# A state-space layer and an attention block on one core: reciprocals in pieces, reordered sends and earlier loads

## The reference, cut to what matters

```python
q = heads(einsum('bsh,oh->bso', x, q_weight) * q_dc)
k = heads(einsum('bsh,oh->bso', x, k_weight) * k_dc)
v = heads(einsum('bsh,oh->bso', x, v_weight) * v_dc * s2)
attn = softmax(einsum('bhqd,bhkd->bhqk', q, k) * scale)
out = einsum('bhqk,bhkd->bhqd', attn, v)          # "attended"
out = einsum('bsh,oh->bso', out, w_weight) * w_dc + skip
```

## Time and profile before

| | |
|---|---|
| three runs | 3378.05, 3388.91, 3394.20 us (median 3388.91) |
| profiled execution | 3385.69 us; its span, first to last instruction, 3383.9 us |
| PE busy | 3030.4 us (90% of the span) |
| DVE busy | 2196.9 us (65%) |
| ACT, POOL busy | 1125.4 us, 1131.3 us (33% each) |
| mean granted clock of PE | 0.909 of full speed |
| attention | about 2294 to 3256 us of the span |
| output stage | about 3256 us to the end |

### The profile page before, as it was taken

One profiled execution on the slowest core, in us unless ns is written; L12 is line 12 of the kernel. 1 busy time (PEld: TensorE's weight loads), 2 busy tenths in 40 slices (PEclk: granted clock), 3 DMA queues, 4 the chain that ended last, 5 costly groups with the idle time before them and its releaser, 6 DMA issues. The chain is left out here.

```text
span 3383.9 us, 55574 instructions
## 1 busy us (share of the span) xinstructions
PE 3030.4 (90%) x20298; PEld 1424.9 (42%) x20298; DVE 2196.9 (65%) x3117; ACT 1125.4 (33%) x1944; POOL 1131.3 (33%) x462
## 2 busy tenths in 40 slices
PE   6888875599999999999984999996999999999979
PEld 3555554234444444444432666672333333323324
DVE  3766663478898989898954334427677666666514
ACT  3645542011111111111112122213666565656620
POOL 0111111113333333333312101102666676666620
PEclk9978865578999999999996999996999999999989
DMA  2333224435555555555543333336334434353354
GB/s 68 129 110 137 90 107 137 128 79 138 143 154 146 150 144 151 144 150 145 149 141 111 128 135 142 145 116 176 83 88 102 100 93 115 73 127 90 76 190 146
DMA packets 248554, 420.82 MB, mean 124 GB/s; under 512 B 51736, under 2 KB 117912, under 8 KB 242024
## 3 DMA queue, kind: packets, MB, share of 16 engines
q1 hardware_dynamic: 202344, 385.61, 39.4%
q10 hardware_dynamic: 46080, 33.57, 4.8%
HBM read 257.82 MB, written 160.98 MB: 124 GB/s over the span
## 5 line engine op out<-in xcount | busy, mean ns | idle before, releaser
L491 DVE CUSTOM_DVE_ANT_0 b_h<-b_h,b_bx,b_bounds_all 128x256 f32<-128x256 f32 x2048 | 966.1, 535 | 145.0 <-PE b_bx L604 144.9
L1208 DVE TENSOR_REDUCE e_half_max<-ef_banks 128x4 f32<-128x2048 f32 x256 | 586.1, 2293 | 289.5 <-PE ef_banks L1161 289.5
L1342 POOL TENSOR_TENSOR e_pair_sum<-e_probs 128x2048 f32<-128x2048 f32 x128 | 585.2, 4572 | 474.7 <-PE ef_banks L1200 270.6
L1318 ACT ACTIVATE e_probs<-ef_banks 128x512 f32<-128x512 f32 x1024 | 555.8, 595 | 374.5 <-PE ef_banks L1175 374.4
L1175 PE MATMUL ef_banks<-e_qs,e_ks 97*128 97x512 f32 x1024 | 393.4, 465 | 23.1 <-DMA e_qs<-e_max_t 19.2
L614 PE MATMUL b_y_psum<-b_h,b_c_weights 128*32 128x128 f32 x8224 | 343.6, 287 | 2.4 <-ACT b_y_stage L654 2.4
L604 PE MATMUL b_bx<-b_x_moving,b_b_weights 24*128 24x512 f32 x1024 | 266.0, 514 | 56.2 <-DMA b_x_moving<-xn_parts 43.9
L1175 PEld LDWEIGHTS ef_banks<-e_qs,e_ks 97*128 97x128 f32 x1024 | 159.7, 195 | 365.3 <-ACT e_probs L1318 304.7
L525 PE MATMUL b_gate<-b_w_gate,b_x_tile 128*128 128x512 f32 x512 | 308.2, 686 | 3.7 <-DMA b_w_gate<-in_w_in_t_dram 3.7
L654 ACT COPY b_y_stage<-b_y_psum 128x128 f32<-128x128 f32 x256 | 67.9, 265 | 728.2 <-PE b_y_psum L614 726.3
L534 PE MATMUL b_p_out<-b_w_out,b_yg_t 128*128 128x512 f32 x512 | 279.1, 637 | 10.3 <-ACT b_yg_t L547 10.3
(11 more groups left out here) (183 smaller groups left out, 3273.3 us busy)
## 6 DMA issues: line engine op xcount, KB each, us to landing
b_x_moving<-xn_parts SPq DMA_DIRECT2D x256, 128.0 KB
e_ks<-qk_parts SPq DMA_DIRECT2D x48, 512.0 KB, 8.0
e_qs<-qk_parts SPq DMA_DIRECT2D x96, 256.0 KB, 11.6
xn_full<-a_xn SPq DMA_DIRECT2D x32, 512.0 KB, 2.6
xn_parts<-a_hi SPq DMA_DIRECT2D x64, 256.0 KB, 2.4
xn_parts<-a_lo SPq DMA_DIRECT2D x64, 256.0 KB, 2.4
b_x_moving<-xn_parts SPq DMA_DIRECT2D x256, 64.0 KB
silu_gate<-b_sg ACTq DMA_DIRECT2D x64, 256.0 KB, 3.6
```

The lines of the kernel that those rows point to most:

```text
L491: return nc.vector._custom_dve(bass.dve_ops.TENSOR_ADD_SAT, **operands)
L1208: nc.vector.tensor_reduce(out=half_max[:, u // UNITS % 2, :, r // NH, r % NH], in_=(banks[:, u % 2 * GROUP:(u % 2 + 1) * GROUP] if u < FIR ...
L1318: nc.scalar.activation(probs[:, g % 4, h, :], p_exp[h % 2], ACT.Exp).then_inc(exps, 1)
L1342: nc.gpsimd.tensor_tensor(out=pair_sum[:, t % 2], in0=probs[:, (2 * t) % 4], in1=probs[:, (2 * t + 1) % 4], op=ALU.add).then_inc(paired, 1)
```

## The change

Four edits.

1. The reciprocal of the sums, 512 columns in one instruction, becomes four instructions of 128 columns. The copy out of PSUM (`take_den`) stays behind unit 79 (143, 207); the pieces follow behind units 80, 81, 82 and 83. Each piece counts `den_inverted` up by one, and `store_rden` waits for all four.
2. In SP's program for a group, `send_max(2n + 2)` moves ahead of `load_rd(m + 1)` and the stores of attended values. `store_rden`, `load_rd(m)` and `send_max(2n + 1)` stay in their places.
3. The matrices of groups 0 and 1 for `max_unit` (four loads of 512 KB) are loaded in `proj_phase`, in batch 3 at `s = 8`; the attention doesn't load them or wait for them.
4. The load of attended batch 0 moves from the end of the attention into SP's program for group 15, and in `out_phase` SP waits until batch 1 has landed before it issues the loads of batches 2 and 3.

```diff
@@ proj_phase, SP
+                        if s == NQ and not ahead:
+                            for i in range(2):
+                                sp.wait_ge(qk_out[i], START + 64)
+                            for i in range(4):
+                                sp.dma_start(mats_ahead[:, i, :].bitcast(f32), QK[2 * (i % 2)].rearrange("b (g r) s -> (b g) r s", r=P)[i // 2]).then_inc(ahead_in, 16)
...
+                sp.wait_ge(ahead_in, START + 64)
@@ attention_phase
         def store_rden(sp, b):
-            sp.wait_ge(den_inverted, START + b + 1)
+            sp.wait_ge(den_inverted, START + (b + 1) * QUARTERS)
...
-            if r == 0:
-                pe.wait_ge(mats_in[i], START + (n // RING + 1) * MATS)
+            if r == 0 and n >= RING:
+                pe.wait_ge(mats_in[i], START + n // RING * MATS)
...
-        def invert(dve, b):
+        def take_den(dve, b):
             dve.wait_ge(key_sums, START + (b + 1) * LANES * NQ)
             if b:
-                dve.wait_ge(den_inverted, START + b)
+                dve.wait_ge(den_inverted, START + b * QUARTERS)
             nc.vector.tensor_copy(den[:], p_d).then_inc(den_taken, 1)
-            dve.wait_ge(den_taken, START + b + 1)
-            if b:
-                dve.wait_ge(rden_out, START + b * RDENS)
-            nc.vector.reciprocal(out=rden[:], in_=den[:]).then_inc(den_inverted, 1)
+
+        def invert(dve, b, quarter):
+            if quarter == 0:
+                dve.wait_ge(den_taken, START + b + 1)
+                if b:
+                    dve.wait_ge(rden_out, START + b * RDENS)
+            cols = slice(quarter * HALFQ // QUARTERS, (quarter + 1) * HALFQ // QUARTERS)
+            nc.vector.reciprocal(out=rden[:, cols], in_=den[:, cols]).then_inc(den_inverted, 1)
@@ attention_phase, SP
-                load_mats(sp, 0)
...
-                load_mats(sp, 1)
...
+                    if n + 1 < NGROUPS:
+                        send_max(sp, 2 * n + 2)
+                    else:
+                        sp.wait_ge(unit_scores, START + ALL_STEPS)
+                        for i in range(LANES):
+                            sp.wait_ge(raw_out[i], START + 16 * ((LANES - 1 - i) // SLOTS + 1))
+                        sp.dma_start(mats[:].bitcast(f32), OT[0:PER_BATCH].rearrange("g p s -> p g s")).then_inc(first_in, 16)
                     if m >= 0:
                         load_rd(sp, m + 1)
                         store_o(sp, m)
                     if NH * n >= LAST:
                         store_o(sp, NH * n)
-                    if n + 1 < NGROUPS:
-                        send_max(sp, 2 * n + 2)
                 store_o(sp, LAST - 1)
-                sp.wait_ge(unit_scores, START + ALL_STEPS)
-                for i in range(LANES):
-                    sp.wait_ge(raw_out[i], START + 16 * ((LANES - 1 - i) // SLOTS + 1))
-                sp.dma_start(mats[:].bitcast(f32), OT[0:PER_BATCH].rearrange("g p s -> p g s")).then_inc(first_in, 16)
                 store_o(sp, HALVES - 1)
@@ attention_phase, DVE
-                    done = u + 1 - AHEAD - LATER
-                    if done > 0 and done % (PER_BATCH * STEPS) == 0:
-                        invert(dve, done // (PER_BATCH * STEPS) - 1)
+                    batch, after = divmod(u + 1 - AHEAD - LATER, PER_BATCH * STEPS)
+                    if batch > 0 and after == 0:
+                        take_den(dve, batch - 1)
+                    if batch > 0 and 1 <= after <= QUARTERS:
+                        invert(dve, batch - 1, after - 1)
@@ out_phase, SP
                 for t in range(3, NQ):
                     load_x2(sp, t)
+                sp.wait_ge(b_in[1], START + 16)
                 load_batch(sp, 2)
                 load_batch(sp, 3)
```

More of the change, by code:

```diff
@@ L736, in _, with proj_phase @@
                     act.wait_ge(sg_out[i], START + LOOPS * 16)
-def proj_phase(nc, I, X1, QK, V, X2, WDC):
+def proj_phase(nc, I, X1, QK, V, X2, WDC, mats_ahead):
     NP = 2 * NK
@@ L760, in proj_phase @@
         consts = sem("consts"); styles = sem("styles"); act_setup = sem("act_setup"); sums = sem("sums"); dve_setup = sem("dve_setup"); rows_in = sem("rows_in"); row_in = sem("row_in")
-        x_in = [sem(f"x_in{i}") for i in range(NQ)]
+        ahead_in = sem("ahead_in"); x_in = [sem(f"x_in{i}") for i in range(NQ)]
         scaled = sem("scaled"); stats_ready = sem("stats_ready"); moments_ready = sem("moments_ready"); var_ready = sem("var_ready"); std_ready = sem("std_ready"); shift_ready = sem("shift_ready"); xl_ready = sem("xl_ready")
@@ L1078, in attention_phase @@
     LATER = 4
+    QUARTERS = 4
     RING = 2
@@ L1451, in build @@
     scan_phase(nc, I, Xp, Xn, Bp, Pd, Iv, Cm, Y, SG, X1, pre_semaphores)
-    proj_phase(nc, I, X1, QK, V, X2, WDC)
     with ExitStack() as ctx:
+        mats = ctx.enter_context(nc.sbuf_tensor("ef_mats", [P, 2 * NH, SEQ], f32r))
+        proj_phase(nc, I, X1, QK, V, X2, WDC, mats)
         w_out = ctx.enter_context(nc.sbuf_tensor("ef_w_out", [P, NK, MODEL], f32))
         w_row = ctx.enter_context(nc.sbuf_tensor("ef_w_row", [P, BATCH, MODEL], f32))
-        mats = ctx.enter_context(nc.sbuf_tensor("ef_mats", [P, 2 * NH, SEQ], f32r))
         banks = ctx.enter_context(nc.psum_tensor("ef_banks", [P, 8, 512], f32))
```

## The result

The changed kernel is slower, by about half a per cent: median 3398.56 us (20 runs, 3375.8 to 3417.8) against 3382.40 us (20 runs, 3370.0 to 3397.6). The ratio is 1.005, with a 95% interval of 1.003 to 1.0069: +17 us, between +10 and +23. The prediction was 3412 us, +26.7 on its profiled execution, and 3394 to 3430. The sign and the mechanism of the stall were right; the size is too large, by some 10 us of the median.

A forecast was written before the change was run, and what follows sets the result against it. PE, busy 90% of the span, was taken as the bound. The terms 20.9 + 11.2 - 5.9 + 0.5 gave +26.7 us on the profiled 3385.7: 3412 us, with 3394 to 3430 to hold 8 in 10.

The forecast's parts named there:

- C: Start of DVE's copy of the sums, 2562.42 in group 4; the zero from which the stall's times were counted.
- step 72: PE's first step of a group's second half, groups 4, 8, 12; predicted start C + 22.1, against C + 13.5 in group 4.
- the sum by the rows: SP's chain from reciprocals ready to the first matmul waiting for the maximum: 4.21 + 3.59 + 0.04 = 7.84 us.
- the 1.9 us more: Estimated extra for the three stalls if each DMA landing costs the page's 2.0 us, not 1.68; not booked.
- The late sends: Edit 2: all nine waits (19.2 us) are for send_max(2n + 1), which stays; moving the even sends gains nothing.
- The cover of the first matrices: Attention start, edit 3: DVE's memset of ks hides the 14.0 us wait; gain 0, up to 9 us without it.
- Predicted -5.9: Edit 4, attention's end: without the late load the output stage begins 5.9 us sooner (5.0 to 6.5).
- +0.5: Output stage, edit 4's new wait holding back loads 2 and 3: +0.5 us, bounds 0 and +2.1.
- The clock after each stall: Low PE clock behind the stalls in groups 4, 8 and 12: 3.7 us each, +11.2 in all (4.6 to 17.9).
- The forecast's 20.9 us: Edit 1: step 72 later by 8.6, 6.5 and 5.8 us, the three removed 2.06 us waits already taken off.
- the prediction's third rival: Stalls without clock loss, PE's clock back by step 73 or low elsewhere before: 3401 us, inside forecast's range; no separate chance.
- its terms' own ends: Range from adding the terms' lower and upper ends, given as 3404 to 3429 us, before the runs' spread.

The follow-up runs named there:

- the kernel that waits for no maximum: Changed kernel with the second half's maximum sent ahead of the stack loads, store_rden and load_rd(m); ratio 0.9817, -62 us against the kernel before.
- edit 1 alone: Kernel before plus only the reciprocal in four pieces, with store_rden waiting for all four; ratio 1.0073 to the kernel before, +25 us.
- the kernels with the memsets on POOL: Versions with the ks memsets moved from DVE to POOL; maximum sent behind the stacks 0.9866, ahead of them 0.9789, ahead with one reciprocal 0.9823.
- edits 2 to 4: Changed kernel with edit 1 undone (one reciprocal); ratio 0.9963 to the kernel before, -12 us.
- two pieces: Kernel before with the reciprocal in two pieces of 256 columns, behind units 80 and 81; ratio 1.0013, +4 us.
- sent ahead at batches: Changed kernel with the second half's maximum sent ahead of store_rden in groups 4, 8 and 12 alone; ratio 0.9925 to the kernel before, -25 us.
- without the wait for batch 1: Changed kernel with one reciprocal and no wait for batch 1 before load_batch 2 in the output stage; output stage 129.8 us.
- sent behind the stacks: Changed kernel with the second half's maximum sent right behind the stack loads in every group, ahead of store_rden and load_rd(m); ratio 0.9900, -34 us.

## Why the prediction was right, and where it was off

**Edit 1, the stall: right to a quarter of a microsecond.** Predicted: a piece 0.95 us, reciprocals ready at C + 14.3, step 72 at C + 22.1, a stall of 10.7 us. Found: 0.94, 14.25, 22.09 and 10.46. From the fourth piece's end to the step is 7.84 us, as the sum by the rows had it. The Trainium skill, "DMA: Bandwidth & Descriptors" (Anatomy of one DMA), gives its 2.0 us for the path of DMAs that GpSimd issues; SP issues these, and the 1.9 us more that the prediction estimated by that figure did not come. Two pieces moved the point as the same sum said, and the send ahead of the inverse sums removed it.

**Edits 2 and 3: right, nothing.** The late sends are those of second halves, and their waits stayed (17.4 us in eight, without the three stalls). The cover of the first matrices was the memsets, as said; the upper bound of 9 us without them was 8.2 (36.0 less 27.8).

**Edit 4: right in the main.** Predicted -5.9, found -6.5 to the first output matmul. For the wait for batch 1 the prediction took +0.5; the output stage was 1.8 longer in this profile and 0.8 longer in the mean of all, and the run without the wait doesn't put it down to that.

**The clock: right behind the stalls, too high over the whole.** The term is "The clock after each stall ... three times: +11.2 us (4.6 to 17.9)". Behind the stalls the figure was good: counted step by step against the kernel that waits for no maximum, the changed kernel lost 1.7, 4.3 and 7.0 us behind the three, and with edit 1 alone 1.7, 3.7 and 4.3: a mean of 3.8, where 3.7 was booked. But the sum also took the rest of the low clock to stay as it was, and the kernel before had much of it. It had twelve waits of PE in the attention (nine for a maximum, three of 2.06 us for DVE), none over 3.4 us, and the clock fell behind most of them. Take the 860.0 us of the kernel without any wait for a maximum or for DVE as the floor. What is left of each profile's attention after floor and waits is low clock (the kernels with the memsets on POOL begin the stage otherwise and are left out):

| profile | attention | waits | low clock |
|---|---|---|---|
| before | 914.9 | 19.2 + 6.2 | 29.5 |
| after | 946.2 | 48.8 | 37.4 |
| edit 1 alone | 941.9 | 50.7 | 31.2 |
| edits 2 to 4 | 919.0 | 23.3 + 6.2 | 29.5 |
| two pieces | 935.1 | 34.0 + 0.7 | 40.4 |
| sent ahead at batches | 911.4 | 18.8 | 32.6 |
| without the wait for batch 1 | 911.1 | 21.1 + 6.2 | 23.8 |
| sent behind the stacks | 882.8 | 11.8 | 11.0 |

The forecast's 20.9 us had already taken off some 4.3 us of low clock that the kernel before had at step 8 of groups 8 and 12, so what it says of this table is 11.2 less 4.3: a low clock 6.9 us above the kernel before's. The profiled pair has 7.9, edit 1 alone 1.7. One execution can't tell these apart: two kernels with the same attention program, edits 2 to 4 and the one without the wait for batch 1, differ by 5.7.

The runs say more, since each has its mean granted clock on record. Time times (1 - clock) is an estimate of what an execution lost to the low clock. With edit 1 alone the mean is 318.4 us, against 306.7 for the kernel before on the same chip: 11.7 more. The changed kernel has 309.9, the one without edit 1 300.6: 9.3 more. But in the profiles 21 to 22 us of the three stalls themselves pass at the low clock, and half of that, about 11 us, is in each of these differences. So outside the stalls edit 1 added about nothing, give or take 8 us: what was lost behind the stalls, less was lost at other waits. By waits alone the sum is 48.8 - 25.4 = +23.4 us, then -6.5 and +1: +18, and the medians say +17 (10 to 23). That is nearest to the prediction's third rival, "the stalls come without the clock loss", 3401 us, by its second reason, that the clock was low in other places before. It is the likely account and not a shown one: the forecast's 6.9 is just inside what the runs leave open, and why less should be lost elsewhere is not known.

That the profiled pair gave +26.5, almost the forecast, is luck: that run was the slowest of 20, and the 20 runs go from 3375.8 us at a mean granted clock of 0.916 to 3417.8 at 0.904. One sum of the prediction is off by 1 at both ends: its terms' own ends give 3403 to 3430, not 3404 to 3429.

**What stays open.** Edits 2 to 4 measured -12 us (-23 to -2), where their own gain in the profile is 5 to 6. Of the 12, some 6 are less low clock by the same estimate (300.6 against 306.7), which is within its uncertainty of 9. If the -12 is real, edit 1 costs 29 us beside them and not 25, and part of the forecast's excess of 10 lies in edits 2 to 4 and not in the clock. More runs would tell.

## What to carry to other kernels

When an instruction is cut into pieces to keep one engine fed, its completion moves as far back as the last piece; look at once for who waits for the completion, and on a queue in program order for everything behind that waiter, whether or not it needs the result. Order a queue by when things are needed: four small DMAs of 2 KB that gate the next half go ahead of megabytes that the next group needs. Sent first, in group 5, they still let the last load of the next group's stacks land 15.6 us before that group began (at 2641.2 and 2656.8 us). A wait of PE can cost more than its length: here, in one pair of profiles, removing 11.8 us of waits gave 22.8.

## What the runs showed of the hardware that was not expected

The time lost to low clock behind a wait hardly depended on how long the wait was: 1.7 to 7.0 us behind the six waits of 10.5 us, 1.5 to 5.9 us (mean 3.3) behind 21 waits of 1.6 to 3.4 us in the kernel before, the changed one and the one with edit 1 alone; two of them are in the earlier trace rows. Behind the four shorter ones there, of 0.7 to 1.4 us, nothing was lost. The first DMAs behind 3.5 MB of queued loads take longer to issue: the four sends of a maximum took 5.67 us there and 2.41 ahead of the loads, and the four loads of inverse sums 8.88 us there and 1.97 elsewhere.
